# A graph layer with residual layer norm on one core: blocks of one low and three high node groups, edge rounds alternating between two halves of the edge list

## What is computed

```python
msg = concat([x[src], edge_attr], axis=1) @ W1 + b1        # 96 -> 128
agg = segment_sum(msg, dst, num_segments=N)
out = layernorm(x + concat([x, agg], axis=1) @ W2 + b2)    # 192 -> 64, no gain or bias
```

## Time and profile before

| | us |
|---|---|
| median of 3 runs (lowest to highest) | 696.72 (695.69 to 697.64) |
| the profiled execution | 697.21 |
| its span, first to last instruction | 695.4 |
| PE / PEld busy | 556.4 / 505.8 |
| DVE busy | 457.0 |
| POOL busy | 425.1 |
| ACT busy | 394.6 |

### The profile page before, as it was taken

How to read it: one execution, slowest core, us unless ns; L and a number is a source line. 1 busy time by engine, 2 the same in 40 slices (tenths; PEclk the granted TensorE clock), 3 DMA queues, 4 the chain that set the end, 5 groups by cost and what they waited for, 6 DMA issues and landing times. The chain is left out here.

```text
span 695.4 us, 27785 instructions
## 1 busy us (share of the span) xinstructions
PE 556.4 (80%) x8394; PEld 505.8 (73%) x8395; DVE 457.0 (66%) x1148; ACT 394.6 (57%) x2012; POOL 425.1 (61%) x419
## 2 busy tenths in 40 slices
PE   1367898988799898898799898889888888873764
PEld 1355788888698897888688897878777777763653
DVE  2687567776657776666657776665788878762443
ACT  0002378887678887777668888776554455532101
POOL 5777737777777777777777777777775454000000
PEclk9957599999989999999989999999999999985665
DMA  2112245455355456546355546544433334220002
GB/s 64 34 36 42 65 134 135 121 153 158 91 153 158 118 134 158 129 123 158 91 146 151 134 131 158 129 122 108 113 92 85 83 83 102 79 60 7 1 1 61
DMA packets 168745, 71.33 MB, mean 103 GB/s; under 512 B 61570, under 2 KB 162447, under 8 KB 168720
## 3 DMA queue, kind: packets, MB, share of 16 engines
q1 hardware_dynamic: 104592, 51.74, 25.8%
q0 software_dynamic: 12544, 12.87, 8.4%
q10 hardware_dynamic: 51584, 6.41, 5.9%
HBM read 45.37 MB, written 25.60 MB: 102 GB/s over the span
## 5 line engine op out<-in xcount | busy, mean ns | idle before, releaser
L393 POOL DMA_INDIRECT feat<-in_x,src_idx x392 | 417.9, 1066 | 159.1 <-issue 121.0
L619 ACT ACTIVATE square<-ps_y 128x64 bf16<-128x64 f32 x784 | 162.7, 239 | 99.1 <-PE ps_y L497 97.0
L506 PEld LDWEIGHTS ps_y<-z_window,onehot 128*128 128x128 bf16 x5664 | 188.5, 99 | 40.8 <-DVE z_window L842 15.6
L506 PE MATMUL ps_y<-z_window,onehot 128*128 128x64 bf16 x5664 | 200.2, 195 | 15.3 <-DVE z_window L842 14.8
L847 DVE TENSOR_TENSOR onehot<-node_of_col,dst_in_group 128x2048 bf16<-128x2048 bf16 x98 | 120.1, 1225 | 78.1 <-issue 68.7
L619 ACT ACTIVATION_READ_ACCUMULATOR square<-ps_y 128x1 f32 x784 | 159.5, 224 | 0.0
L497 PE MATMUL ps_y<-wx,x_t 128*128 128x128 f32 x784 | 117.0, 294 | 26.5 <-ACT x_t L611 23.7
L497 PEld LDWEIGHTS ps_y<-wx,x_t 128*128 128x128 f32 x784 | 99.3, 199 | 31.4 <-ACT x_t L611 28.0
L429 PE MATMUL ps_z<-wz,feat_t 97*128 97x64 f32 x784 | 104.7, 292 | 13.4 <-DVE z_rest L748 13.4
L842 DVE COPY z_window<-z 128x384 bf16 x472 | 115.2, 295 | 0.0
L578 ACT ACTIVATE feat_t<-ps_t 97x512 f32<-97x512 f32 x98 | 58.6, 598 | 98.5 <-PE ps_z L429 72.5
(11 more groups left out here) (125 smaller groups left out, 270.2 us busy)
## 6 DMA issues: line engine op xcount, KB each, us to landing
xin<-in_x SPq DMA_DIRECT2D x97, 256.0 KB
out<-yout SPq DMA_DIRECT2D x97, 256.0 KB
feat<-in_x,src_idx POOLq DMA_INDIRECT x392
feat<-in_edge_attr ACTq DMA_DIRECT2D x96, 64.0 KB
z<-in_src SPq DMA_DIRECT2D x1, 192.0 KB
z<-in_dst SPq DMA_DIRECT2D x1, 192.0 KB
xin<-in_x SPq DMA_DIRECT2D x1, 128.0 KB
out<-yout SPq DMA_DIRECT2D x1, 128.0 KB
```

Source lines behind the costliest of these rows:

```text
L393: nc.gpsimd.indirect_dma_start(out=feat[h][:, feat_at(k) + feat_slot(c), 0:C], out_offset=None, in_=x[:, :], in_offset=bass.IndirectOffset ...
L506: mm = nc.tensor.matmul(ps_y[h][:, col:col + C], onehot[h][:, g, s, a, :], z_window[h][:, g, s, part * C:(part + 1) * C], start=False, sto ...
L619: sq = nc.scalar.activation(square[:, q, :], ps_y[h][:, q * C:(q + 1) * C], ACT.Square, accum_out=sumsq[:, h, q:q + 1])
```

## The change

- Block b is no longer four neighbouring groups. Group 0 is one group of the low quarter of the nodes (0 to 25,087, `LOW`), groups 1 to 3 are three neighbours of the rest; both go downwards with b. The x load and the store of a block are two DMAs each, and SP's loop is written out.
- Chunks keep the order of the edge list. Even rounds work eight chunks of the lower half, from chunk 192 down to 0, odd rounds eight of the upper half, from 384 down to 200 (`chunk_at`).
- The low group takes three chunks at first, the three others two: nine slots a block in place of eight. The two further chunks (`second`) are now for the low group alone, and set if it has over three chunks or any group needs the loop. The loop is as before, for any group.
- `need` is now counted in rounds, from the table of firsts, for the low half and the upper half apart. `lacking`, `AHEAD`, `units` and LAG stay.
- `z_rest` moves from SBUF to PSUM, constants and the lookup `picks` get a third row.

The diff, cut to its core:

```diff
+LOW = BLOCKS * GN
+HIGH = G - 1
+LOW_ROUND = PAIRS // 2
+HIGH_CHUNK = (LOW_ROUND + 1) * 2 * CB
+SLOTS = 3 + 2 * HIGH
+TAKEN = (3, 2, 2, 2)
+SLOT = (0, 3, 5, 7)
+LOOP_FROM = (5, 2, 2, 2)
...
+        def low_part(t, b):
+            at = (BLOCKS - 1 - b) * GN
+            return t[at:at + GN, :].rearrange("(p a) c -> p (a c)", p=P, a=A)
+        def high_part(t, b):
+            at = LOW + (BLOCKS - 1 - b) * HIGH * GN
...
+        def chunk_at(k):
+            at = k % 2 * (2 * CB * LOW_ROUND + CB) + (2 * CB * LOW_ROUND - CB * k)
...
+                sp.dma_start(xin[h][:, 0, :], low_part(x, b)).then_inc(x_loaded[h], 16)
+                    sp.dma_start(xin[h][:, 1:G, :], high_part(x, b)).then_inc(x_loaded[h], 16)
...
                 pe.wait_ge(hot_ready, b + 1)
                 for g in range(G):
                     pe.wait_ge(window_ready, G * b + g + 1)
-                    pair_sum(g).then_inc(group_summed, 1)
+                    mm = slots_sum(g, TAKEN[g])
+                    if g == 0:
+                        mm.then_inc(low_summed, 1)
                 with pe.If(second > 0):
-                    for g in range(G):
...
+                    slots_sum(0, 2)
...
-            nc.gpsimd.iota(round_chunks[:, :], pattern=[[2 * CB, PAIRS]], base=0, channel_multiplier=0,
+            nc.gpsimd.iota(round_chunks[:, :], pattern=[[1, PAIRS]], base=0, channel_multiplier=0,
...
-            link(nc.vector.tensor_scalar(need[:, :], first[:, :], 3.0, None, ALU.add))
-            link(nc.vector.tensor_tensor(need[:, :], need[:, :], last[:, :], ALU.max))
+            link(nc.vector.tensor_scalar(last[:, :], last[:, :], -1.0, None, ALU.add))
+            link(nc.vector.scalar_tensor_tensor(out=far_first[:, :], in0=first[:, :], scalar=4.0, in1=last[:, :],
+                                                op0=ALU.add, op1=ALU.max))
+            link(nc.vector.tensor_scalar(first_round_i[:, :], steps[:, 0:G], 3, None, ALU.arith_shift_right))
+            link(nc.vector.tensor_copy(first_round[:, :], first_round_i[:, :]))
+            link(nc.vector.tensor_scalar(need[:, :], first_round[:, :], -2.0, float(2 * LOW_ROUND + 1), ALU.mult, ALU.add))
+            link(nc.vector.scalar_tensor_tensor(out=need[:, :], in0=first[:, :], scalar=float(HIGH_CHUNK),
+                                                in1=need[:, :], op0=ALU.is_lt, op1=ALU.mult))
+            link(nc.vector.tensor_scalar(first_round[:, :], first_round[:, :], float(LOW_ROUND + 1), -2.0, ALU.max, ALU.mult))
+            link(nc.vector.tensor_scalar(first_round[:, :], first_round[:, :], float(2 * PAIRS), None, ALU.add))
+            link(nc.vector.scalar_tensor_tensor(out=far_first[:, :], in0=far_first[:, :], scalar=float(HIGH_CHUNK),
+                                                in1=first_round[:, :], op0=ALU.is_ge, op1=ALU.mult))
+            link(nc.vector.tensor_tensor(need[:, :], need[:, :], far_first[:, :], ALU.max))
             link(nc.vector.reduce_max(block_need[:, :], need[:, :], axis=AX.X))
-            link(nc.vector.tensor_scalar(block_need[:, :], block_need[:, :], 1.0, None, ALU.add))
...
-                    for g in range(G):
-                        dve.wait_ge(group_summed, G * b + g + 1)
+                    dve.wait_ge(low_summed, b + 1)
```

More of the change, by code:

```diff
@@ L232, in feat_at, with cut_part, transfers @@
             return k % 2 * CB
[L234 to L257, removed]
+        def low_part(t, b):
[3 more added lines that the diff above has]
+            at = LOW + (BLOCKS - 1 - b) * HIGH * GN
+            groups = HIGH if b > 0 else 1
+            return t[at:at + groups * GN, :].rearrange("(g p a) c -> p g (a c)", g=groups, p=P, a=A)
+        def cut_part(t):
+            return t[CUT:N, :].rearrange("(p a) c -> p (a c)", a=A)
+        def transfers(k, h):
+            return 2 * k + (1 if h == 0 and k > 0 else 0) if isinstance(k, int) else 2 * k + (1 - h)
+        ea_batches = edge_attr[0:(BATCHES - 1) * BATCH_EDGES, :].rearrange("(b k p) c -> b p k c", k=CB, p=P)
+        ea_last = edge_attr[LAST_EDGES:E, :].rearrange("(k p) c -> p k c", p=P)
+        def chunk_at(k):
+            at = k % 2 * (2 * CB * LOW_ROUND + CB) + (2 * CB * LOW_ROUND - CB * k)
+            if isinstance(k, int):
+                return at
+            return nc.s_assert_within(at, 0, CHUNKS - 2 * CB, skip_runtime_bounds_check_because="rounds end with the last")
         def wait_rounds(eng, semaphore, k, per_round=1):
@@ L295, in _ @@
             sp.dma_start(units_row[:, 2:PAIRS], scratch[n_steps + 2:n_steps + PAIRS].rearrange("(o n) -> o n", o=1)).then_inc(s_loaded_steps, 16)
[L298 to L301, removed]
             def free_yout(k, h):
[L304 to L306 removed]
+                if k > 0:
+                    sp.wait_ge(out_stored[h], 16 * transfers(k, h))
@@ L553, in _ @@
                 message(1, h)
-            for s, bank in enumerate((ps_x[1], ps_b)):
+            for s, (bank, groups) in enumerate(((ps_x[1], G), (ps_b, G), (ps_x[0], 1))):
                 for t in range(4):
-                    pe.wait_ge(s_picks, 4 * s + t + 1)
-                    mm = nc.tensor.matmul(bank[:, 0:BLOCKS * G], dst_ckf[:, t, :], picks[:, s, t, :], start=(t == 0), stop=(t == 3))
+                    pe.wait_ge(s_picks, 4 * s + t + 1 if s < 2 else 12)
+                    mm = nc.tensor.matmul(bank[:, 0:BLOCKS * groups], dst_ckf[:, t, :], picks[:, s, t, 0:BLOCKS * groups],
+                                          start=(t == 0), stop=(t == 3))
                 mm.then_inc(s_picked, 1)
@@ L870, in one_hots @@
                                     turn_no = dve.snap(pairs_done)
-                                    chunk = nc.s_assert_within(dve.snap(firsts[g] + 2 * n), 0, CHUNKS - 6, skip_runtime_bounds_check_because="the table of steps ends every range before the last chunk")
+                                    chunk = nc.s_assert_within(dve.snap(firsts[g] + 2 * n), 0, CHUNKS - 2 - LOOP_FROM[g], skip_runtime_bounds_check_because="the table of steps ends every range before the last chunk")
                                     for s in range(2):
```

298 lines of the change are left out of this document (151 added, 147 removed).

## The result

The changed kernel takes 952.99 us, median of four runs (952.48 to 953.87), against 696.45 us of the kernel before: 1.3683 times as long, 95% interval 1.3659 to 1.3706. The forecast was 990 us with a range of 935 to 1,065. The profiled execution took 952.72 us, 1.8 us more than its span of 950.9.

What follows compares the result with a forecast made beforehand. Gathers were taken to set the pace until 585 us, with 110 us of tail. For the changed kernel 518 + 372 + 36 + 48 + 6 + 9 = 989 us of span, so 990 us, range 935 to 1,065.

Steps and rivals of the forecast that it cites:

- The step that decides: Unit table: block 0's low group reaches chunk 200, needs 48 rounds, so nearly all units run after all edges; chance 0.76.
- (1): Edge phase: 392 gathers from 14.6 us, one per 1.25 us, ending at 505 us; at 1.395 us each, 57 us more.
- (2): After the last gather: the last two messages with their splits on ACT and DVE, 13 us, to 518 us.
- (3): Unit phase: 49 units without edge rounds at 7.6 us each, 372 us; taken between 7.1 and 8.05 + 0.5.
- DVE near 90% busy: Sign of a right forecast: DVE near 90% busy while the one-hots run in some 470 us with POOL silent.
- (4): Further chunks in the unit phase: 18 blocks at 2.0 us each, 36 us; lower end 1.0 each, 18 us.
- (5): Loops in the unit phase: 20 pairs in 7 blocks, 1.55 us a pair and 2.5 a block, 48 us.
- (6): First unit at the low clock, 6 us, and the end after the last loop's last one-hot, 9 us.
- (A): Rival: the gate of block 0 stays open, units run beside gathers, about 647 us, faster by 7%; chance 0.08.
- (B): Rival: gate closes, units slowed to 9.5 us by loads and stores or SP's issues, 1,083 us; chance 0.12.
- (C): Rival: PE stays at 1.2 GHz in the unit phase, units take 13.9 us, 1,298 us in all; chance 0.03.

Runs made afterwards that it cites:

- e1: Changed kernel plus bounds checks on loaded table entries, low group's first chunk capped at 195 (gate open): 1,074.35 us, 1.0096 times the kernel before beside it.
- f1: Repeat on another chip of the changed kernel with bounds checks and first chunk capped at 195: 1,079.33 us, 1.0058 times the kernel before beside it.
- g1: Another repeat of the changed kernel with bounds checks and first chunk capped at 195: 1,079.13 us, 1.0030 times the kernel before beside it.
- e2: Kernel before plus bounds checks, need of block 0 set so that it lacks until round 48 (gate closed): 1,116.22 us.
- f2: Repeat of the kernel before with bounds checks and block 0 held until round 48: 1,118.00 us.
- f4: Changed kernel plus bounds checks, with two unused one-hots on DVE in each edge round: 1,085.37 us.
- f5: Changed kernel plus bounds checks, with SP loading 200 times 256 KB into yout during the edge phase: 1,090.97 us.
- h1: Changed kernel plus bounds checks, first chunk capped at 195, units run four at a time: 1,112.49 us, 1.0367 times the kernel before beside it.
- g0: Kernel before, with only on-chip bounds checks of the loaded unit-table entries added: 1,080.97 us, 1.0052 times the kernel before beside it.
- c0: Changed kernel, with only on-chip bounds checks of the loaded unit-table entries added: 1,108.35 us, beside 1,065.61 for the kernel before.

## Why the prediction was right, and where it was off

**The step that decides held.** The forecast rested on one number, worked out from the input: block 0 has f = 196, f + 4 reaches 200, need 48. In the trace no unit runs before the edges are done; with f = 195 in e1, f1 and g1 the units start at 92 to 95 us; with the need put into the kernel before by hand (e2, f2) the order is the same. For the order of the work, cause and effect are shown both ways. How many of the 256 us between 696 and 953 an open gate would save is not measured; the traces show that 425 us of the span now come behind the last edge work.

**The sum**, 989 us forecast and 950.9 measured, term by term:

- (1) Edge phase, 505 forecast, 508.9 measured: +4. A gather takes 0.945 us and comes every 1.26 in the mean ((507.99 - 14.40) / 391), 1.25 in most, which makes the 4 us; the end of the range at 1.395 did not apply. What I left open there, f4, f5 and the sorted gathers settle: one-hots and the normalising on DVE lengthen the gathers, window copies and loads do not. The section on separate sides in the Trainium skill (SBUF — State Buffer, section "SBUF: two separate sides") says this not only of DVE's two-port modes, on which I drew, but also of a DVE operation with two SBUF inputs beside a GpSimd operation that reads SBUF, and it says that a transfer and a compute operation don't slow each other. The 1.97 us beside one-hots (two SBUF inputs) agree with the first, the 0.946 us beside 164 GB/s with the second.
- (2) The last splits, 13 forecast, 526.03 - 508.93 = 17.1 measured: +4. DVE waits 7.5 and 5.0 us for ACT, and PE's messages take some 3.6 us at half clock.
- (3) Units, the mis-sized term: 7.6 us each forecast, 6.89 to 6.93 measured, 49 x 6.91 = 339 in place of 372: -33. DVE's work was right (1.36, 0.81 and 1.29 against 1.38, 0.86 and 1.29), and so was ACT's chain of 6.9 us. What failed is the step from there: I put half a us on top because two units in a row beside gathers had taken 8.05, and kept the bare sum only as a lower end, 7.1. With POOL silent the 0.65 us behind the reciprocal did not occur. The measured unit is even under my lower end, by 0.2: each row is a little under its forecast (windows 0.81 for 0.86, one-hot 1.36 for 1.38, gaps 0.90 and 0.33 for 0.95 and 0.35), and the reciprocal starts 0.05 us before the windows end. The sign "DVE near 90% busy" failed with it: DVE was busy 254 of 320 us in the unit phase, 79%. This term lies below its own lower end and the whole time still in the range, because that end took further chunks and loops at their least too.
- (4) Further chunks, 2.0 us a block forecast. A unit with two such blocks took 854.08 - 844.25 = 9.83 us between its stores, so (9.83 - 6.93) / 2 = 1.45 us a block, 26 for 18: -10. Units with one such block grew by 1.22 (8.15). I take it that part of L888's time lies under PE's sums, which subtracting three one-hot pairs from the old block could not show.
- (5) and (6) Loops, first unit and end, 63 forecast: 424.9 - 339 - 26 = 60, -3. In the last block a pair takes (938.99 - 931.44) / 5 = 1.51 us, 1.55 forecast.

4 + 4 - 33 - 10 - 3 = -38, and 989 - 38 = 951. No error was saved by another of its size; one wrong unit time makes most of the miss.

**The rivals.** (A), the open gate: not what happened. Whether it would have been 647 us on the chip of the first profiles stays open, since no experiment ran under conditions in which the kernel before takes 697. On the other chips it lies 0.3 to 1.0% above the kernel before, so there its promise did not show. (B), slower units by transfers or SP's issues: wrong. SP issues eight DMAs a unit at 0.34 to 0.48 us, some 3.4 us of 6.93, and the DMA engines were at 0.54 with 153 GB/s. (C), the low clock in the unit phase: wrong, 1.00 from 560 to 880 us. By the rule of the Trainium skill on streams that wait for data in each step, for longer than they compute (TensorE: Matmul & The Clock Gate, section "HAM oscillation — how this bites in real kernels") it would hold if DVE left waits in each unit; PE's block sums waited for windows only 13 times, 13.2 us in the whole kernel, so the rule had nothing to bite on.

**Left open.** What the idle time called issue and remote is. The runs show that it goes with passages between edge rounds and units (f1 against h1), that it moves between PE and ACT, that it isn't there in a row of units, and that the comparisons of bounds are not its cause (g0). A slow supply of instructions where an engine jumps would fit all of this, but nothing here shows it. More transfers of instructions it is not: the two queues that the pages call instruction moved 25 packets, 0.31 MB, in the kernel before at 697 us and the same 25 in g0, with 292 gaps in PE's block sums; c0 has 28, f1 29.

## What to carry to other kernels

Where a table orders the work, compute the table for the real input before costing any instruction: here one block with a need of 48 put 425 us of work behind the edges, where the ninth slot costs 8 us. A requirement that is the maximum over "might be touched" chunks, and bounds all later blocks through the first one, wants a look at its values at the seams. When two rings are nearly tied, cost a phase by the bare ring with the neighbours that it will have, not by a row in which the other phase runs beside it.

## What the runs showed of the hardware

- PE's granted clock was 0.50 from 70 to 500 us, with PE busy 201 of the 360 us from 120 on, and 0.97 in the same stretch before, with 318 of 360. From 30 to 70 us it was 0.99, with PE busy 23.6 of 40 us. The low level cost the gathers nothing, since POOL waited for PE only 0.6 us in all.
- A gather's time depends on DVE and not on loads: 0.94 us alone, up to 2.1 us beside one-hots (f4), 0.95 us beside 164 GB/s (f5). It matters where DVE's inputs lie: gathers that start in `z_lows` took 1.34 us with `z_rest` in SBUF and 0.94 with `z_rest` in PSUM.
- The same kernel took 697 us where it was first profiled and 1,066 to 1,076 beside the experiments (1,081 with the comparisons, g0), while units in a row took the same in the changed kernel and in c0, to 0.5 us in 425. A comparison between two kernels holds on the chip where it was made, and can have another size on the next: closed gate against the kernel before was 1.37 in the first conditions and 1.04 in the second.
